# Second attention of a two-layer decoder: a new written order of calls on TensorE, VectorE and ScalarE

## What is computed

```
q = (x @ wq.T).reshape(B, T, 32, 8); k, v the same with 8 heads (each serves 4 query heads)
q, k = rope(q), rope(k)
scores = einsum('bhtd,bhsd->bhts', q, k) / sqrt(8) + causal mask
y = softmax(scores) @ v                      # softmax over s
return y.reshape(B, T, 256) @ wo.T
```

## Time and profile before

| what | us |
|---|---|
| median of three runs | 824.19 |
| the profiled execution | 830.23 |
| its span | 828.2 |
| PE busy in the span | 776.9 (94%) |
| DVE, ACT, POOL busy | 515.1, 345.9, 358.4 |
| mean granted clock of PE | 0.975 |

### The profile page before, as it was taken

One profiled execution on the slowest core, in us unless ns is written; L12 is line 12 of the kernel. 1 busy time (PEld: TensorE's weight loads), 2 busy tenths in 40 slices (PEclk: granted clock), 3 DMA queues, 4 the chain that ended last, 5 costly groups with the idle time before them and its releaser, 6 DMA issues.

```text
span 828.2 us, 13217 instructions
## 1 busy us (share of the span) xinstructions
PE 776.9 (94%) x4432; PEld 598.0 (72%) x4432; DVE 515.1 (62%) x1010; ACT 345.9 (42%) x814; POOL 358.4 (43%) x333
## 2 busy tenths in 40 slices
PE   6899999999979989999999997889888898999997
PEld 5788888888854457888888886555556444788886
DVE  5666677667678966333333338576786698864535
ACT  3556564646552052322323234346677102534332
POOL 3221212114107933655555546376775796522100
PEclk9999999999998989999999999779999999999999
DMA  9310101010200113443434332000000012000001
GB/s 320 71 52 25 51 25 51 25 51 25 65 20 32 32 55 95 122 127 91 133 91 126 98 90 76 1 9 2 1 2 2 25 51 70 1 17 17 1 1 51
DMA packets 27457, 45.52 MB, mean 55 GB/s; under 512 B 3632, under 2 KB 17008, under 8 KB 27152
## 3 DMA queue, kind: packets, MB, share of 16 engines
q1 hardware_dynamic: 27408, 44.88, 18.4%
HBM read 43.52 MB, written 1.18 MB: 54 GB/s over the span
## 4 chain that ended last, share of the span: by engine, by line
PE 76%; DVE 8%; POOL 7%; ACT 5%; issue 3%; DMA 1%; SPq 0%; DVEq 0%; ACTq 0%; POOLq 0%
PE bank L1727 11%; PE bank L1729 11%; PE bank L1728 11%; PE bank L1765 4%; PE bank L1766 4%; PE bank L1767 4%; POOL arena L648 4%; PE bank L1752 3%; PE bank L2339 3%; PE bank L1794 2%; PE bank L1796 2%; PE bank L1798 2%; PE bank L2065 1%; PE bank L2253 1%; PE bank L2260 1%
## 5 line engine op out<-in xcount | busy, mean ns | idle before, releaser
L1727 PE MATMUL bank<-xTh,ringh 128*128 128x512 f32 x420 | 169.0, 402 | 1.0 <-DVE xTl L1300 0.5
L1728 PE MATMUL bank<-xTl,ringh 128*128 128x512 f32 x420 | 165.8, 395 | 0.0
L1729 PE MATMUL bank<-xTh,ringl 128*128 128x512 f32 x420 | 165.8, 395 | 0.0
L1373 DVE TENSOR_TENSOR arena<-bank,arena 128x512 f32<-128x512 f32 x48 | 33.2, 691 | 114.7 <-ACT arena L989 105.6
L1729 PEld LDWEIGHTS bank<-xTh,ringl 128*128 128x128 f32 x420 | 79.1, 188 | 18.8
L1727 PEld LDWEIGHTS bank<-xTh,ringh 128*128 128x128 f32 x420 | 79.3, 189 | 17.2 <-issue 2.3
L1728 PEld LDWEIGHTS bank<-xTl,ringh 128*128 128x128 f32 x420 | 79.2, 189 | 15.0
L696 POOL TENSOR_TENSOR arena<-arena 128x512 f32<-128x512 f32 x48 | 62.5, 1303 | 52.0 <-DVE HTl L1377 49.3
L989 ACT ACTIVATE arena<-bank 128x512 f32<-128x512 f32 x48 | 28.7, 598 | 126.0 <-PE bank L1729 126.0
L613 POOL CAST ringh<-ring 128x768 fp32r<-128x768 f32 x15 | 13.2, 878 | 149.7 <-DMA ring<-w_attn 149.7
L1765 PE MATMUL bank<-outh,HTh 128*128 128x256 f32 x192 | 54.9, 286 | 3.0 <-DVE outl L1190 1.2
(11 more groups left out here) (316 smaller groups left out, 1892.6 us busy)
## 6 DMA issues: line engine op xcount, KB each, us to landing
ring<-w_moe SPq DMA_DIRECT2D x24, 256.0 KB, 2.9
arena<-route SPq DMA_DIRECT2D x16, 384.0 KB, 4.1
ring<-w_attn SPq DMA_DIRECT2D x15, 384.0 KB, 3.2
toep<-toep SPq DMA_DIRECT2D x32, 128.0 KB, 2.1
arena<-route SPq DMA_DIRECT2D x16, 256.0 KB, 4.3
outring<-w_down SPq DMA_DIRECT2D x24, 128.0 KB, 2.0
outring<-wo_attn SPq DMA_DIRECT2D x16, 128.0 KB, 2.1
arena<-route SPq DMA_DIRECT2D x16, 128.0 KB, 4.0
```

What stands on the lines that cost most here:

```text
L1727: pe.matmul(o, ringh[:, slot, wc], xTh[:, k, halves[j]], start=(k == 0), stop=False)
L1728: pe.matmul(o, ringh[:, slot, wc], xTl[:, k, halves[j]], start=False, stop=False)
L1729: ins = pe.matmul(o, ringl[:, slot, wc], xTh[:, k, halves[j]], start=False, stop=(k == DK - 1))
```

## The change

The loops over couples are written out call by call on four engines, and the calls stand in another order on PE, DVE and ACT. The functions that issue instructions are nearly the same: `norm_y` is cut into `divide_y` and `scale_y`, which always follow each other; `project_out(b)` for two batches becomes `project_pair(q)`, so that its 8 matmuls stand together; the copy of the values waits for `v_psum` of 2, since both halves of `values` now count it up. Instructions, shapes, buffers and waits are else those of before.

```diff
-            def norm_y(y):
+            def divide_y(y):
 ...
                 dve.reciprocal(yr[:], at[:, :, :, HD]).then_inc(y_rec, 1)
+            def scale_y(y):
...
@@ DVE
-            for d in range(1, COUPLES):
-                t = PER * d
-                add_mask(t)
-                maximum(t - 2)
...
-                if d in (4, 6):
-                    add_pair((d - 4) // 2)
+            maximum(3)
+            maximum(4)
             split_x(1, 1)
+            take_values()
+            add_mask(6)
+            maximum(5)
+            add_mask(7)
+            turn_keys(1)
...
+            scale_y(7)
+            maximum(34)
+            add_pair(0)
+            add_mask(36)
+            maximum(35)
+            add_mask(37)
+            add_mask(38)
+            add_mask(39)
+            maximum(36)
+            divide_y(8)
...
@@ ACT
-            for t in range(TILES):
...
-                if t >= 2:
-                    evac_pt(t - 2)
...
-                act.wait_ge(shifted, t + 1)
-                act.activation(probs[t % 12], probs[t % 12], ACT.Exp, scale=HD ** -0.5).then_inc(exp1_done, 1)
+            exp_probs(33)
+            evac_pt(30)
+            evac_y(8)
+            exp_probs(34)
+            evac_pt(31)
+            exp_probs(35)
+            evac_pt(32)
+            evac_pt(33)
+            exp_probs(36)
...
@@ PE
-            def project_out(b):
-                q = b // 2
+            def project_pair(q):
                 pe.wait_ge(yt_evac, q + 1)
-                for k in range(DK):
...
+                for b in (2 * q, 2 * q + 1):
+                    for k in range(DK):
...
+            scores_late(6)
+            weigh(8)
+            turn_probs(31)
+            turn_probs(32)
+            turn_y(8)
+            turn_probs(33)
+            turn_pair(1)
+            scores_early(6)
+            weigh(9)
+            turn_probs(34)
+            turn_probs(35)
+            turn_y(9)
+            turn_probs(36)
+            project_pair(1)
+            scores_late(7)
```

More of the change, by code:

```diff
@@ L770, in shift_scores, with place_values @@
                     .then_inc(shifted, 1)
-            for t in range(TILES):
[L773 to L789, removed]
+            def place_values():
+                pool.wait_ge(yn_done, 1)
+                for j in range(2):
+                    first = j * (VZ - 32)
+                    ins = pool.tensor_copy(Vz[0][j][0:LATE, :], Vn[0:LATE, first:first + VZ])
+                ins.then_inc(vz_low, 1)
@@ L1043, in evac_pair, with exp_probs @@
                 act.activation(yT[q % 2].rearrange("p k b t -> p (k b t)"), bank[:, 5 + q // 3, :], ACT.Copy).then_inc(yt_evac, 1)
[L1045 to L1048, removed]
-                if t >= 2:
-                    evac_pt(t - 2)
[L1051 to L1056, removed]
+            def exp_probs(t):
@@ L2132, in _ @@
             values(0, B // 2)
[L2133 to L2176, removed]
@@ new lines, in _ @@
+            scores_late(1)
+            project_keys(1)
+            turn_probs(1)
+            turn_probs(2)
+            choose_keys(1, 0)
+            turn_probs(3)
+            scores_early(1)
+            choose_keys(1, 1)
+            turn_probs(4)
+            turn_probs(5)
+            turn_probs(6)
+            scores_late(2)
+            weigh(0)
+            turn_probs(7)
+            turn_probs(8)
+            turn_y(0)
+            turn_probs(9)
+            scores_early(2)
+            weigh(1)
@@ new lines, in _ @@
+            turn_probs(10)
+            turn_probs(11)
+            turn_y(1)
+            project_queries(1, 0, 0)
+            turn_probs(12)
+            scores_late(3)
+            project_queries(1, 0, 1)
+            weigh(2)
+            turn_probs(13)
+            turn_probs(14)
+            turn_y(2)
+            turn_probs(15)
+            project_queries(1, 1, 0)
+            scores_early(3)
+            weigh(3)
+            turn_probs(16)
+            turn_probs(17)
+            turn_y(3)
@@ new lines, in _ @@
+            project_queries(1, 1, 1)
+            turn_probs(18)
+            scores_late(4)
+            weigh(4)
+            turn_probs(19)
+            turn_probs(20)
+            turn_y(4)
+            turn_probs(21)
+            turn_pair(0)
+            scores_early(4)
+            weigh(5)
+            turn_probs(22)
+            turn_probs(23)
+            turn_y(5)
+            turn_probs(24)
+            project_pair(0)
+            scores_late(5)
+            weigh(6)
+            turn_probs(25)
@@ new lines, in _ @@
+            turn_probs(26)
+            turn_y(6)
+            turn_probs(27)
+            scores_early(5)
+            weigh(7)
+            turn_probs(28)
+            turn_probs(29)
+            turn_y(7)
+            turn_probs(30)
+            scores_late(6)
[9 more added lines that the diff above has]
+            turn_probs(35)
```

449 lines of the change are left out of this document (359 added, 90 removed).

## The result

The changed kernel takes 820.78 us (median of 10 runs, 819.55 to 822.14), the kernel before 824.24 in the same job (10 runs, 823.47 to 831.17): a ratio of 0.9952, 95% interval 0.9931 to 0.9973. That is 3.5 us less, a gain that is clear of the noise but about half of the 1% that the prediction asks for before it speaks of faster, and 2.1 us over the forecast of 818.7. The profiled execution took 821.02 us with a span of 819.0 and a mean granted clock of 0.986; PE is busy 767.6 us, DVE 508.0, ACT 345.0, POOL 358.2.

What follows compares the result with a forecast made beforehand. PE bounds the stage where it has work, else the chain scores, mask, maxima, shift, exp, turn. Terms 1.9 + 3.5 + 1.6 = 7.0 us, less 1.4, say 5.5, off 824.19 give 818.7 us; range 812 to 826.5.

Steps and rivals of the forecast that it cites:

- case A: Whole kernel: 818.7 us, the clock stays up at the start and ACT's new order gives part back; chance 0.48.
- Late scores 2 to 7: Five couples of the stage: 55.4 us in sum against 58.9, 3.5 us gained, 5.7 us of waits left.
- short prices: Per-call times a little short: 0.2 us off for each of seven couples, 7.0 - 1.4 = 5.6 us.
- Start: Up to late scores 2: waits for exp(4) and exp(5) go, waits around the keys come; 1.9 us gained.
- I take the same gain from it: Last step: the 5.5 us gain, read from the profiled execution, taken off the median, 824.19 - 5.5 = 818.7 us.
- LS7 to pair: Late scores 7 to the last pair: 21.9 us in place of 23.5, 1.6 us gained.
- B: ACT's gating costs little, PE's work alone sets the pace: 5 us more gained, 813.7 us; chance 0.20.
- C: The clock falls at the start all the same: 3 us less gained, 821.7 us; chance 0.24.
- D: Slower: PE waits at nearly every tile, the clock falls again and again; four falls bring 832.7 us; chance 0.08.

Runs made afterwards that it cites:

- evac_earlier: The changed kernel with each evacuation of a turned tile k ahead of exp(k + 3) instead of behind it, ACT's list alone; 817.47 us, ratio to before 0.9900.
- the second trace: The kernel before, unchanged, profiled once more; 823.49 us.
- start: The changed kernel with `turn_keys(1)` right behind the values on DVE and `evac_keys(1, 0)` ahead of an evacuation on ACT; 821.08 us, ratio to before 0.9964.
- all: The changed kernel with evac_earlier and start together, and `turn_queries(1, 0, 1)` ahead of a value block on DVE; 817.17 us, ratio to before 0.9916.
- before_new_act: The kernel before with ACT's list of the changed one, `evac_keys(1, 1)` moved behind exp(10); 854.38 us, ratio 1.0372.
- max4_first: The kernel before with DVE's maxima of tile 4 ahead of the split of x; 823.97 us, ratio 0.9984.

## Why the prediction came out as it did

**The new order: case A, as forecast.** Late scores 2 to 7 take 55.62 us, forecast 55.4; PE is busy 50.08 of them, forecast 49.7; the waits are 5.5, forecast 5.7. The couples are 10.18, 13.31, 11.29, 8.87 and 11.97 us, forecast 10.45, 13.1, 11.3, 8.6 and 11.95. With the 0.2 us a couple for short prices the forecast was 56.4, so the prices were short by 0.2 us in all five couples and not by 1.0. Couple 6 waits 0.43, 0.42 and 0.84 us, forecast 0.75, 0.5 and 0.6 at tiles 32, 33 and 36; `weigh(12)` waits 1.04, forecast 1.3. The evacuation was named as the cause of all these, and `evac_earlier` takes the first two away, leaves 0.34 of the third, and gives 4.0 us from LS1 to the pair.

**Start.** The waits were forecast as 0.7, 1.8 and 0.7 us and are 0.64, 1.61 and 0.65. Early scores 1 come 7.59 us behind late scores 1 (546.67 less 539.08); forecast was 7.5 (549.5 less 541.99). LS1 to LS2 is 11.80 us, forecast 553.55 less 541.99 = 11.56.

**Where the gain comes from: not as forecast.** The prediction put PE's work from late scores 2 to 7 at 49.7 us in either order, so that 9.2 of the 58.9 us were waits and low clock, and 3.5 of these were to be won. Both kernels have a trace with that stretch at full clock, before first, then changed:

```profile
550.44:607.61 57.17, 51.50 (x606) 33.45 (x606) 44.05 (x84) 39.15 (x73) 42.10 (x41) 1.00 0.01 2
550.88:606.50 55.62, 50.08 (x609) 33.86 (x608) 44.51 (x85) 40.41 (x76) 45.02 (x44) 1.00 0.01 2
```

PE is idle for 5.67 and 5.54 us there. Of the 1.55 us gained only 0.1 is idle time; 1.4 us is PE with less busy time for nearly the same matmuls (a `choose_keys` has gone out of this stretch and one batch's projection has come in, some 0.95 us each). It is so over the whole stretch from LS1 to the pair: 931 and 932 matmuls, named waits of 11.7 us in both, PE busy 81.25 us before and 77.54 now. At most 1.7 of these 3.7 us is the fall of the clock (a mean of 0.87 over 12.74 us, some 3.3 us at 1.2 GHz). The rest, 2.0 or more, I read as turned tiles standing in pairs: two in a row take 0.93 us from start to start, one alone mostly 0.5 to 0.66, and the changed kernel has 16 places with two or more in a row where the second trace has 6. No run tries this apart. So the new order moved PE's waits and did not shorten them. The forecast of the new order was right; what it said was lost in the old one was not, and its 5.7 us of waits left were what the old order had already.

**The mis-sized step of the sum is the last one: "I take the same gain from it".** Against the trace that the terms were read from, the stretch from LS1 to the pair gained 95.82 - 89.48 = 6.3 us, near the sum of 5.6. Against the second trace, whose time (823.49) is near the median, it gained 93.41 - 89.48 = 3.9:

| stretch | forecast, raw | against the first trace | against the second |
|---|---|---|---|
| LS1 to LS2 | 1.9 | 1.6 | 0.9 |
| LS2 to LS7 | 3.5 | 3.3 | 1.6 |
| LS7 to pair | 1.6 | 1.4 | 1.4 |

The difference is the fall of the clock, 10 us long in one trace and about 3 in the other. The forecast counted the whole of it as something the new order wins from every execution. With 2.4 us less, 5.5 would have been 3.1, and the medians differ by 3.5. That 818.7 lies near the measured time is thus in part luck: the long fall added 2.4 us, and the 1.4 us taken off for short prices, of which about 0.6 was needed, took some of it back. The two profiled executions near the medians differ by only 2.5 us in span: the changed kernel's stage began 1.4 us later (530.35 against 528.98). Nothing ahead of that was changed, and kernels that share all code up to there begin at 529.11 (`evac_earlier`) and 530.37 (`start`), so that is taken as chance; the clock from 515 to 530 is 0.89 in both, and the cause is open.

**The rivals.** B (gating costs little) fell: the waits are there and cost 4 us. It saw where time was left but put it too high: with the gating gone, `evac_earlier` comes out 7.3 us under its before, B said 10.5. C and D fell in the changed kernel's trace: the clock is 1.00 from 530 to 634, and in the traces of `start`, `evac_earlier` and `all` it is 1.00 from 530 to 600 too. PE waited 1.61 us ahead of `choose_keys` and more than fifteen times up to 1.04 us behind it, all at 2.4 GHz. By the rule of the Trainium skill, "TensorE: Matmul & The Clock Gate", section "A second HAM failure mode: psum-queue depth-cycling", such a stage could swing between both levels; the trace does not agree. What D describes did happen in `before_new_act`, with six falls in the stretch. What the kernel before had ahead of its fall were two waits in a row, 1.35 and 1.34 us in the second trace, with 0.66 us of work between them. In the changed kernel no such pair is left. That this is the reason the clock holds was not tried apart; `max4_first`, with 0.63 and 1.95, still fell, and `start`, with 1.42 and 0.36 and the early scores between them, did not. And in `before_new_act` the clock also fell, at 597 and 628, behind two shorter waits (0.97 and 0.93 us at 597) with 0.66 us of work between them. Why the clock holds in the changed kernel stays open.

## What to carry to other kernels

The lists of engines that run in order fit each other or cost: a list is to be judged beside the others, and on its own neither ACT's nor DVE's told what it was worth. Where a gain comes from is told by the busy and idle time of the engine in one stretch of both traces at the same clock: here the waits that one saw vanish had only moved. An evacuation that frees a bank belongs ahead of an exp that may be late, wherever the next turned tile needs the bank. A term that holds a low clock is to be looked up in a second trace before it is taken off a median; the clock column of two executions of the same kernel, side by side, tells what is the kernel's and what the execution's.

## What was not expected of the hardware

The same kernel, unchanged, had the clock at 1.2 GHz for 10 us in one execution and for a little over 3 us in another, behind waits of 2.08 and 1.34 us in the one and 1.35 and 1.34 us in the other. Whether the longer first wait made the longer fall no run here shows. And lists that don't fit cost far more than the few us that were expected: 30 us for ACT's list beside the old ones, 15 us for DVE's old list beside the new ones. PE's added waits are 21.7 and 11.5 us of that, and most of the rest fits the falls of the clock that come with them.
